# Post-norm attention and an int8 product: last heads joined by transfers, one more chunk in single steps

## The chip, the cores and the metric

The kernel runs on one core of a Trainium2 chip. The metric is device microseconds of one launch; the median of three runs of the kernel before is 1008.3 us (1007.88 to 1009.81). Engines as the profile calls them: PE (TensorE, matmuls; PEld its weight loads), DVE (VectorE), ACT (ScalarE), POOL (GpSimd), SP (SyncE, which issues all the transfers here).

## The reference

The input `x` has shape (2, 2048, 256), with 16 heads of width 16.

```python
Q, K, V = proj(Wq), proj(Wk), proj(Wv)            # x @ W.T, split into heads
O = flash_attention(Q, K, V, block 128, causal)   # online softmax, float32
x = layernorm(x + O @ Wo.T)                       # over the 256 features
# quantised product: integers of both sides, scales put back on
lhs_scale = max(absmax over a token, 1e-12) / 127
rhs_scale = max(absmax over a column, 1e-12) / 127
y = (round(x / lhs_scale) @ round(rhs / rhs_scale)) * lhs_scale * rhs_scale
x = layernorm(x + y)
```

## The kernel before

**Groups and steps.** Four heads of one batch are a group; there are eight groups, four for each batch, and they run one after the other. In a group the 2048 queries are cut into four chunks of 512, and a chunk meets the keys in blocks of 128, only those at or before it. That makes 4 + 8 + 12 + 16 = 40 steps (chunk c, block kb), numbered from 0 in each group; `NS` is 40 and `FIRST[c]` = 0, 4, 12, 24 is a chunk's first step. In the last four steps of a chunk the block lies on the diagonal, and the widths are 512, 384, 256 and 128. A step makes four score products (one for each head, into one of three PSUM banks `ps_score`), four exponentials on ScalarE into `PR` (L1003), and, two steps later (`LAG`), the values product into `ps_acc` (L734), whose row for each head also gives the sum of the exponentials.

**Items.** The maximum that each query subtracts is found ahead. TensorE makes scores into `ps_max`, VectorE reduces them (L1072, 1.06 us in the mean); such a piece is an item. Groups one to six make the items of the group that follows (80 each, a few of their own); the seventh makes 88 and the eighth none. `quota` (L164) writes down how many items are done after each score of a group. It goes through the steps with a price for each product and for the end work due in that step, and takes the highest pace at which all items still fit.

**A chunk's end.** When a chunk's last values are in `ps_acc`, ScalarE copies them to `accS` (`copy_acc`, L987), after the fourth exponential of the next chunk's second step. In groups one to seven SP stores these heads to HBM. When the four groups of a batch are through, a chunk's end work can be done: normalise all 256 rows by the inverse sums, project with `Wo`, add `x`, first layernorm, quantise, transpose, integer product, scale, add, second layernorm, store. It is done in halves of 256 tokens. `ENDS` = 8 chunks are numbered m = 0 to 7 over both batches and 16 halves e = 0 to 15.

**Two ways of doing the end work.** The first three chunks (`SOON = 3`) run one group after another beside the attention of the second batch: project, turn and product go through the score banks, ScalarE copies the results out and scales, GpSimd multiplies, and the VectorE steps are single instructions, one in each step (`SOON_DUE`, `gap=1`). The fourth chunk and the whole second batch run late, in the last group (`LATE_DUE`, `gap=0`): banks of `ps_max`, which has no items then; VectorE reads the projection in PSUM, and does all the instructions of a part in one step.

**The joined chunks.** Chunks 4 to 7 (`JOINED`) need the last group's own four heads. Those never go to HBM. The other twelve heads are loaded into `o_in(m)` (192 of the 256 rows; the last 64 rows of the second half are empty). For the last four heads TensorE sums the exponentials by token out of `accS` (`token_sums`, L879), VectorE inverts (`invert_last`, L1215), TensorE spreads the inverses over the rows (`spread_inverses`, L891), VectorE multiplies `accS` in place (`normalise_last`, L1222). The projection (`project`, L854) then has three products for each 128 tokens: 128 rows, 64 rows, and `accS` with `wo_last` (weights in the places of the spread-out heads). For chunk 7 the first two run ahead and `finish_projection` (L904) adds the third.

**What sets the order.** All instructions stand in program order on their engine; a wait stops all that is behind it. The lists `HALF_START`, `CHUNK_DUE` and the `..._DUE` tables give, for each part, the step at which each engine does it. `COPIED` holds the steps at which the copies of the joined chunks are made. In the last group `between_scores` (L775) puts a part of the projection behind each score, the token sums and spreads and the turn behind the first score of a step, the product behind the third, halves of the values behind the second and fourth.

Of the kernel before, what the change touches and what calls it, by code (L numbers as in the profile page):

```python
# [26 lines left out]
P = 128  # L27
# [7 lines left out]
HG = 4  # L35
# [26 lines left out]
def build(nc, x, wq, wk, wv, wo, ffn, out):  # L62
    B, T, D = x.shape
    DH = D // HEADS
# [4 lines left out]
    HALVES = D // P  # L69
    GR = HG * DH  # L70
# [32 lines left out]
    SOON = 3  # L103
# [6 lines left out]
    JOINED = range(CHUNKS, ENDS)  # L110
    COPIED = [LAST_GROUP + FIRST[c] + 1 for c in range(1, CHUNKS)] + [ALL - 1]
    HALF_START = [at for at in SOON_START for s in range(2)] + [LAST_GROUP, LAST_GROUP + 2] + \
        [at for k in COPIED[:-1] for at in (k + 2, k + 4)] + [ALL + 1, ALL + 2]
# [3 lines left out]
        for at in ((-16, -13, -11, -4), (-14, -11, -6, 1), (-13, -9, 2, 8), (-8, -4, 6, 14), (5, 9, 21, 29))]  # L117
# [15 lines left out]
    JOIN_DUE = dict(LATE_DUE, spread=0, normalise=0, project0=1, project1=1)  # L133
    LAST_DUE = dict(LATE_DUE, spread=0, normalise=0, project0=-2, project1=-2, finish=1)
    DUE = [SOON_DUE[e % 2] if e < SOON_HALVES else LATE_DUE if e // 2 not in JOINED else JOIN_DUE if e < 2 * ENDS - 2
# [11 lines left out]
    def joins_due(k):  # L147

        return [m for m in JOINED if HALF_START[2 * m] - 1 == k]

# [111 lines left out]
    with ExitStack() as ctx:  # L262
# [91 lines left out]
        e_token = sem("sums_by_token")  # L354
        e_spread = sem("inverses_spread")
# [40 lines left out]
        joined = lambda m: m - JOINED[0]  # L396
# [36 lines left out]
        with nc.Block() as block:  # L433
            @block.sync
            def _(sp):
# [43 lines left out]
                def end_parts(k):  # L479
                    for m in chunks_due(k, "sums_in"):  # L480
                        sums_in(m)
                    for m in chunks_due(k, "sums_back"):
                        sums_back(m)
                    for m in chunks_due(k, "load"):
                        load(m)
                    for e in due(k, "store"):
                        store_result(e)
# [40 lines left out]
                def load(m):  # L528
# [5 lines left out]
                    for h in range(HALVES):  # L534
# [6 lines left out]
                        .then_inc(e_x[SLOT[m]], 16)  # L541

# [33 lines left out]
            def _(pe):  # L576
# [198 lines left out]
                def between_scores(k, j):  # L775


                    at = NS * (GROUPS - 1) + k
                    project(at, j // 2, j % 2)
                    if j == 0:  # L780
                        joins(at)
                        late_turn(at)
                    if j == 2:
                        late_product(at)
                    if j % 2:
                        values_half(*divmod(at - LAG, NS), j // 2)

# [66 lines left out]
                def project(k, t, h):  # L854


                    for e in late_due(k, f"project{t}"):
                        m, s = divmod(e, 2)
                        if t == 0 and h == 0:
# [3 lines left out]
                            if e == 2 * JOINED[0]:  # L863
                                pe.wait_ge(e_wo, 16 * HG)
                            if m in JOINED and m < ENDS - 1:
                                pe.wait_ge(e_last, LAST_STEPS * joined(m) + 3 + s)
                        at, n = s * HALF + t * P, half_rows(m, h)
# [4 lines left out]
                        last = h == HALVES - 1  # L872
# [31 lines left out]
                def finish_projection(e):  # L904
                    m, s = divmod(e, 2)
                    pe.wait_ge(e_last, LAST_STEPS * joined(m) + 3 + s)
                    for t in range(TPH):
# [25 lines left out]
            def _(act):  # L933
# [53 lines left out]
                def copy_acc(g, c):  # L987
# [3 lines left out]
                    else:  # L991
                        act.wait_ge(e_y, TPH * late(2 * (JOINED[c - 2] + 1)))
                    act.copy(accS[:, c % 2, :], ps_acc[:, :]).then_inc(s_accS, 1)  # L993

                def group(g):
                    for k, (c, kb) in enumerate(STEPS):
                        w = CH - skip(c, kb)
                        for j in range(HG):
# [6 lines left out]
                            if kb == 1 and j == HG - 1 and (g or c):  # L1005
                                copy_acc(g if c else g - 1, (c - 1) % CHUNKS)
# [424 lines left out]
```

## Time and profile before

| | |
|---|---|
| median of three runs | 1008.3 us |
| profiled execution | 1007.38 us, span 1005.7 us |
| busy share of the span | PE 94%, DVE 80%, ACT 72%, POOL 27% |
| mean granted clock of TensorE | 0.983 of full speed |
| groups one to eight, from first exponential to the next group's | 98.3, 98.7, 98.7, 102.9, 104.1, 104.1, 106.7, 121.5 us |
| from the last group's last exponential to the end | 29.8 us |

The group times are differences between the starts of ACT's exponentials (L1003) in the timeline; the last group goes to the end of its last one. In the rows below, a line of the windows gives start:end, length, busy time and instruction count of PE, PEld, DVE, ACT and POOL, granted clock, DMA share and GB/s. A line of the waits gives the waiting engine, tile and line, what released it, and total us, times and longest. A piece of the chain of waits, or of the timeline, begins with its start and its length in us. A line of the groups gives count, busy time, mean ns of one, and idle time ahead of it. A transfer line ends with KB each and the median us from issue to landing.

### The profile page before, as it was taken

Reading aid. Unit: us, or ns where it says so; the run is one execution under the profiler, and the core shown is the slowest. Engines: PE = TensorE matmul, PEld = TensorE weight load, DVE = VectorE, ACT = ScalarE, POOL = GpSimd, SP = SyncE. Lnnn points to the kernel's source line nnn. Section 1 sums busy time; section 2 is a strip of 40 time slices with the busy share of each in tenths; the row PEclk is TensorE's granted clock in tenths of the full one; section 3 lists DMA queues with packets and bytes.
Section 4 is the critical chain, followed back from the end, with each engine's and each line's share of the span. In section 5 each row is a group of like instructions: output and inputs, shape, how many; then the busy total and the mean of one; then the engine's idle time right before and its main releaser. Section 6 shows DMA issues by size and latency. Waiting matters only on the chain.

```text
span 1005.7 us, 41095 instructions
## 1 busy us (share of the span) xinstructions
PE 944.5 (94%) x18208; PEld 590.9 (59%) x18208; DVE 799.5 (80%) x1081; ACT 719.9 (72%) x1494; POOL 272.0 (27%) x443
## 2 busy tenths in 40 slices
PE   8989999999999999999999999999999999879993
PEld 5645556656765676566656675666666654444441
DVE  5488888887888788878889898999899899365426
ACT  3423458788788878887878877887787887757670
POOL 4433452102210221021213230333124212353322
PEclk9999999999999999999999999999999999989995
DMA  5565440002210220022302230124013114502101
GB/s 177 161 200 159 157 125 15 5 9 53 69 32 9 60 68 24 9 58 80 83 6 60 64 116 8 40 76 114 19 34 78 50 33 112 114 14 75 34 2 42
DMA packets 70865, 66.47 MB, mean 66 GB/s; under 512 B 14704, under 2 KB 65200, under 8 KB 70688
## 3 DMA queue, kind: packets, MB, share of 16 engines
q1 hardware_dynamic: 70688, 63.84, 22.8%
q8 instruction: 143, 2.34, 1.0%
q14 instruction: 34, 0.28, 0.1%
HBM read 42.43 MB, written 20.91 MB: 63 GB/s over the span
## 4 chain that ended last, share of the span: by engine, by line
PE 77%; DVE 10%; ACT 6%; SPq 3%; issue 2%; POOL 1%; DMA 1%; POOLq 0%; ACTq 0%; DVEq 0%
PE ps_acc L734 20%; PE ps_score L681 19%; PE ps_max L681 18%; DVE block_max L1072 6%; PE ps_score L604 5%; ACT PR L1003 4%; PE ps_score L611 3%; PE ps_max L824 2%; PE ps_max L679 2%; SPq L439 2%; PE ps_max L699 2%; PE ps_score L824 1%; ACT accS L993 1%; PE ps_acc L585 1%; DVE end_slots L1183 1%
## 5 line engine op out<-in xcount | busy, mean ns | idle before, releaser
L1072 DVE TENSOR_REDUCE block_max<-ps_max 128x2 f32<-128x1024 f32 (+3 forms) x640 | 654.3, 1059 | 113.3 <-PE ps_max L681 56.7
L1003 ACT ACTIVATE PR<-ps_score 128x512 f32<-128x512 f32 (+3 forms) x1280 | 627.2, 539 | 160.4 <-PE ps_score L681 141.7
L681 PE MATMUL ps_score<-QS,KS 99*32 99x512 bf16 (+3 forms) x5120 | 452.3, 350 | 3.3 <-ACT PR L1003 2.2
L734 PE MATMUL ps_acc<-PR,VG 128*32 128x256 f32 (+1 forms) x5104 | 367.7, 350 | 10.5 <-ACT accS L993 9.1
L681 PE MATMUL ps_max<-KS,QS 96*32 96x512 bf16 (+3 forms) x4544 | 335.1, 348 | 5.5 <-DVE block_max L1072 2.9
L681 PEld LDWEIGHTS ps_score<-QS,KS 99*32 99x32 bf16 x5120 | 169.4, 96 | 96.5 <-ACT PR L1003 22.5
L734 PEld LDWEIGHTS ps_acc<-PR,VG 128*32 128x32 f32 x5104 | 170.2, 110 | 83.7 <-ACT PR L1003 16.2
L681 PEld LDWEIGHTS ps_max<-KS,QS 96*32 96x32 bf16 x4544 | 138.5, 96 | 88.4 <-DVE block_max L1072 37.7
L1318 POOL TENSOR_SCALAR_AFFINE_SELECT PR<-PR 128x512 f32<-128x512 f32 x128 | 82.8, 647 | 284.3 <-ACT PR L1003 284.1
L699 PE MATMUL ps_max<-mask_q,ident_b 128*32 128x96 bf16 (+3 forms) x1808 | 99.1, 200 | 0.0
L699 PEld LDWEIGHTS ps_max<-mask_q,ident_b 128*32 128x32 bf16 x1808 | 60.7, 97 | 10.0
L1326 POOL CAST max_parts<-neg_max 16x128 bf16<-16x128 f32 (+1 forms) x30 | 8.9, 297 | 195.1 <-ACT neg_max L985 193.1
L604 PE MATMUL ps_score<-PR,wT 128*128 128x512 f32 x128 | 60.3, 597 | 0.8 <-ACT neg_max L963 0.8
L945 ACT CAST end_slots<-ps_score 128x512 bf16<-128x512 f32 x32 | 18.7, 585 | 56.7 <-PE ps_score L604 56.7
L1305 POOL TENSOR_TENSOR end_slots<-PR,end_slots 128x512 bf16<-128x512 f32 x32 | 37.0, 1155 | 78.3 <-ACT end_slots L950 78.3
L679 PE MATMUL ps_max<-KS,QS 96*128 96x512 bf16 (+3 forms) x144 | 35.9, 345 | 7.1 <-DVE block_max L1072 7.0
L604 PEld LDWEIGHTS ps_score<-PR,wT 128*128 128x128 f32 x128 | 23.3, 190 | 20.6 <-issue 18.0
L1355 POOL TENSOR_SCALAR var_eps<-moments 128x2 f32<-128x2 f32 x32 | 7.4, 231 | 86.3 <-DVE moments L1178 86.3
L611 PE MATMUL ps_score<-wT,PR 128*128 128x256 f32 x128 | 30.0, 381 | 0.0
L1172 DVE BATCH_NORM_STATS2 stats<-end_slots 128x6 f32<-128x256 f32 x48 | 19.0, 417 | 12.0 <-POOL end_slots L1374 11.8
L1121 DVE TENSOR_TENSOR PR<-ps_score,end_slots 128x512 f32<-128x512 f32 x32 | 21.7, 683 | 8.0 <-ACT end_slots L945 6.9
L679 PEld LDWEIGHTS ps_max<-KS,QS 96*128 96x128 bf16 x144 | 13.3, 97 | 24.3 <-DVE block_max L1072 13.1
(125 smaller groups left out, 558.5 us busy)
## 6 DMA issues: line engine op xcount, KB each, us to landing
QS<-qparts SPq DMA_DIRECT2D x192, 64.0 KB, 2.4
KS<-kparts SPq DMA_DIRECT2D x192, 64.0 KB, 2.3
qparts<-end_slots SPq DMA_DIRECT2D x16, 384.0 KB, 3.8
kparts<-end_slots SPq DMA_DIRECT2D x16, 384.0 KB, 3.1
PR<-in_L_attn_x SPq DMA_DIRECT2D x8, 512.0 KB, 4.3
heads_out<-accS SPq DMA_DIRECT2D x112, 32.0 KB
end_slots<-in_L_attn_x SPq DMA_DIRECT2D x6, 512.0 KB, 7.5
out_y<-end_slots SPq DMA_DIRECT2D x12, 256.0 KB, 2.1
```

Source lines behind the costliest of these rows:

```text
L604: m = pe.matmul(bank, wT[:, w, mh, nh * P:nh * P + P], xT[:, n % 2, mh, :], start=mh == 0, stop=mh == HALVES - 1)
L611: m = pe.matmul(bank[:, t * D:t * D + D], xT[:, n % 2, mh, tile * P:tile * P + P], wT[:, 2, mh, :], start=mh == 0, stop=mh == HALVES - 1)
L679: return pe.matmul(bank[:, 0:w], stack, moving, start=True, stop=stop)
L681: m = pe.matmul(bank[t * QW:t * QW + QW, 0:w], stack[:, t * QW:t * QW + QW], moving, start=True, stop=stop)
L699: m = pe.matmul(bank[r:r + QW, w - P + r:w], ident_b[:, r:r + QW], mask_q[:, r:P], start=False, stop=True)
L734: m = pe.matmul(ps_acc[EYE * j:EYE * j + EYE, a:b], VG[:, kb, j, :], PR[:, k % 4, j, a - s:b - s], start=kb == 0 and a == 0, stop=k == LAS ...
L824: y = pe.matmul(out[r:r + QW], stack[:, r:r + QW], moving, start=start, stop=stop)
L1003: act.activation(PR[:, k % 4, j, 0:w], ps_score[:, bank_of(use), 0:w], ACT.Exp, scale=SCALE).then_inc(s_exp, 1)
L1072: dve.tensor_reduce(block_max[:, h * PAIR:h * PAIR + PAIR, i, b], ps_max[:, slot_at:slot_at + PAIR, 0:w], AX.X, ALU.max).then_inc(s_reduce ...
L1121: dve.tensor_tensor(rest[:, q % RESTS, :], ps_score[:, u % 3, :], parts[:, n % 2, u, 0, :], ALU.subtract)\
L1305: pool.tensor_tensor(parts[:, n % 2, u, 2, :], rest[:, q % RESTS, :], parts[:, n % 2, u, 1, :], ALU.subtract).then_inc(part3, 1)
L1318: pool.affine_select(out=block, in_=block, compare_op=ALU.is_ge, fill=0.0, base=0, pattern=[[0, HG], [1, P]], channel_multiplier=-1).then_ ...
```

## The change

- `SOON` is 4: the fourth chunk of the first batch takes the way of the first three. It starts at step 26 of the seventh group and ends at step 23 of the last one. The plan of the items counts this work.
- The joined chunks 4, 5 and 6 start their halves five and seven steps after the step of the copy, where it was two and four. Token sums stay one step after it; both halves are spread two steps after it and normalised three steps after it. Then SP copies the four heads by four transfers of 16 x 512 from `accS` to the empty rows of `o_in(m)` (`join_heads`), and the projection, which waits for these (`e_join`), has two products of 128 rows for each 128 tokens. Its two tiles are made in two steps, where it was one.
- In the last group the turn stands behind a step's fourth score, and token sums and spreads at the end of the step.
- `copy_acc` follows the third exponential of its step, where it was the fourth, in all groups. In the last group its wait for the buffer is for the transfers, where it was for the projection.
- The loads of chunk 7 come five steps later, and its weights' wait moves to `finish_projection`.

```diff
-    SOON = 3
+    SOON = 4
...
-    HALF_START = [at for at in SOON_START for s in range(2)] + [LAST_GROUP, LAST_GROUP + 2] + \
-        [at for k in COPIED[:-1] for at in (k + 2, k + 4)] + [ALL + 1, ALL + 2]
+    HALF_START = [at for at in SOON_START for s in range(2)] + \
+        [at for k in COPIED[:-1] for at in (k + 5, k + 7)] + [ALL + 1, ALL + 2]
...
-        for at in ((-16, -13, -11, -4), (-14, -11, -6, 1), (-13, -9, 2, 8), (-8, -4, 6, 14), (5, 9, 21, 29))]
+        for at in ((-14, -11, -6, 1), (-13, -9, 2, 8), (-8, -4, 6, 14), (5, 9, 26, 33))]
...
-    JOIN_DUE = dict(LATE_DUE, spread=0, normalise=0, project0=1, project1=1)
+    JOIN_DUE = [dict(LATE_DUE, spread=-3, normalise=-2), dict(LATE_DUE, spread=-5, normalise=-4, join=-4)]
...
-        return [m for m in JOINED if HALF_START[2 * m] - 1 == k]
+        return [m for m in JOINED if COPIED[joined(m)] + 1 == k]
...
+                    for e in due(k, "join"):
+                        join_heads(e // 2)
...
+                def join_heads(m):
+
+                    sp.wait_ge(e_last, LAST_STEPS * (joined(m) + 1))
+                    for j in range(HG):
+                        r = P - GR + j * DH
+                        sp.dma_start(o_in(m)[r:r + DH, HALVES - 1, :], accS[EYE * j:EYE * j + DH, m % 2, :])\
+                            .then_inc(e_join, 16)
...
-                    if j == 0:
-                        joins(at)
-                        late_turn(at)
                     if j == 2:
                         late_product(at)
+                    if j == 3:
+                        late_turn(at)
                     if j % 2:
                         values_half(*divmod(at - LAG, NS), j // 2)
+                    if j == 3:
+                        joins(at)
...
-                                pe.wait_ge(e_last, LAST_STEPS * joined(m) + 3 + s)
-                        at, n = s * HALF + t * P, half_rows(m, h)
+                                pe.wait_ge(e_join, 16 * HG * (joined(m) + 1))
+                        at, n = s * HALF + t * P, half_rows(m, h) if m == ENDS - 1 else P
...
-                        y = tiled(rows, o_in(m)[0:n, h, at:at + P], wT[0:n, 3, h, :], h == 0, last and m not in JOINED)
-                        if last and m in JOINED:
-                            y = tiled(rows, accS[:, m % 2, at:at + P], wo_last[:, :], False, True)
-                        if last:
+                        y = tiled(rows, o_in(m)[0:n, h, at:at + P], wT[0:n, 3, h, :], h == 0, h == HALVES - 1)
+                        if h == HALVES - 1:
                             y.then_inc(e_y, 1)
...
-                        act.wait_ge(e_y, TPH * late(2 * (JOINED[c - 2] + 1)))
+                        act.wait_ge(e_join, 16 * HG * (c - 1))
...
-                            if kb == 1 and j == HG - 1 and (g or c):
+                            if kb == 1 and j == HG - 2 and (g or c):
                                 copy_acc(g if c else g - 1, (c - 1) % CHUNKS)
```

## Rows read from the trace of the kernel before

**Rows 1.** The page, part 4: shares of the chain that ended last, by engine.

```profile
PE 77%; DVE 10%; ACT 6%; SPq 3%; issue 2%; POOL 1%; DMA 1%; POOLq 0%; ACTq 0%; DVEq 0%
```

**Rows 2.** Windows: second, sixth, seventh group, seventh's end, last in thirds, tail.

```profile
239.20:337.90 98.70, 96.34 (x2184) 62.93 (x2180) 82.56 (x84) 80.36 (x168) 17.13 (x37) 1.00 0.15 41
643.60:747.70 104.10, 101.74 (x2288) 66.74 (x2292) 93.13 (x125) 84.38 (x180) 29.38 (x53) 1.00 0.22 60
747.70:854.40 106.70, 103.55 (x2300) 63.56 (x2300) 100.42 (x127) 84.91 (x177) 28.37 (x51) 1.00 0.28 72
812.10:854.40 42.30, 41.32 (x849) 22.49 (x841) 41.16 (x46) 31.92 (x63) 6.66 (x12) 1.00 0.33 79
854.40:884.70 30.30, 26.06 (x513) 15.10 (x515) 12.75 (x37) 21.67 (x47) 12.69 (x21) 1.00 0.43 95
884.70:922.80 38.10, 32.63 (x560) 16.74 (x560) 24.56 (x72) 22.59 (x47) 15.02 (x21) 0.87 0.19 51
922.80:975.90 53.10, 48.72 (x852) 24.12 (x844) 22.86 (x69) 41.51 (x90) 16.29 (x24) 0.97 0.07 22
975.90:1005.70 29.80, 12.68 (x122) 7.67 (x120) 17.01 (x54) 3.01 (x5) 10.11 (x16) 0.66 0.11 36
```

**Rows 3.** Waits of all engines in the last group, 854.4 to 975.9.

```profile
ACT PR L1003 <- PE ps_score L681: 34.2, 45, 4.9
...
PE ps_max L899 <- DVE last_sums L1220: 4.0, 1, 4.0
```

**Rows 4.** The chain of waits, 882 to 904: first and last VectorE piece.

```profile
889.80 0.77 DVE stats L1172 x2
...
902.92 0.26 DVE last_sums L1220
```

**Rows 5.** Groups of instructions by line, 854.4 to 975.9.

```profile
L824 PE MATMUL ps_max<-wo_last,accS 128*32 128x256 f32 x96 | 7.7, 391 | 0.0
...
L1051 ACT ACTIVATE V<-V 128x512 bf16<-128x512 f32 x4 | 2.6, 649 | 0.3 <-DVE V L1212 0.3
...
L1226 DVE TENSOR_TENSOR accS<-accS,ps_max 128x256 f32<-128x256 f32 x6 | 2.5, 420 | 20.3 <-PE ps_max L899 20.3
```

**Rows 6.** ScalarE's timeline, 953 to 964.

```profile
955.06 5.99 ACT L1003 ACTIVATE PR<-ps_score 128x512 f32<-128x512 f32 x12 [1.19 <-PE ps_score L681]
```

**Rows 7.** Line 1003 in the last group: shortest/median/longest ns, stretch, shapes.

```profile
L1003 ACT ACTIVATE PR<-ps_score x160: 272/597/727, 854.4 to 975.6; 128x512 f32<-128x512 f32 x112, 128x384 f32<-128x384 f32 x16, 128x256 f32<-128x256 f32 x16, 128x128 f32<-128x128 f32 x16
```

**Rows 8.** SyncE's timeline, 860 to 872: store of heads, last load issued.

```profile
860.32 1.91 SPq L456 DMA_DIRECT2D heads_out<-accS  x4
...
870.83 0.58 SPq L540 DMA_DIRECT2D end_slots<-in_L_attn_x  x1
```

**Rows 9.** Transfers of the whole run.

```profile
QS<-max_parts SPq DMA_DIRECT2D x96, 4.0 KB, 1.7
```

**Rows 10.** Transfers of the stretch 850 to 885.

```profile
V<-in_L_attn_x SPq DMA_DIRECT2D x1, 512.0 KB, 9.2
...
QS<-max_parts SPq DMA_DIRECT2D x3, 4.0 KB, 6.5
```

**Rows 11.** The chain of waits from 249 to 253.5.

```profile
250.38 0.24 PE ps_acc L734 x2
...
251.01 0.59 ACT accS L993
...
251.73 0.64 PE ps_acc L734 x8
```

**Rows 12.** Waits before the last group, 140.9 to 854.4.

```profile
PE ps_acc L734 <- ACT accS L993: 9.1, 21, 0.6
```

**Rows 13.** VectorE's timeline, 962 to the end.

```profile
973.65 0.75 DVE L1172 BATCH_NORM_STATS2 stats<-end_slots 128x6 f32<-128x256 f32 x2 [7.44 <-POOL end_slots L1374]
...
974.60 0.84 DVE L1248 SCALAR_TENSOR_TENSOR end_slots<-ps_max,lscale,ffn_scale 128x256 f32<-128x256 f32 x2
```

More of the change, by code:

```diff
@@ L110, in build @@
     JOINED = range(CHUNKS, ENDS)
+    joined = lambda m: m - JOINED[0]
     COPIED = [LAST_GROUP + FIRST[c] + 1 for c in range(1, CHUNKS)] + [ALL - 1]
-    HALF_START = [at for at in SOON_START for s in range(2)] + [LAST_GROUP, LAST_GROUP + 2] + \
-        [at for k in COPIED[:-1] for at in (k + 2, k + 4)] + [ALL + 1, ALL + 2]
+    HALF_START = [at for at in SOON_START for s in range(2)] + \
+        [at for k in COPIED[:-1] for at in (k + 5, k + 7)] + [ALL + 1, ALL + 2]
     soon_chunk = lambda at: dict(sums_in=at - 17, sums_back=at - 14, load=at - 7, outputs=at - 2)
@@ L132, in build @@
                     take=7, product=8, scale=9, residual2=10, rstd2=12, store=14)
-    JOIN_DUE = dict(LATE_DUE, spread=0, normalise=0, project0=1, project1=1)
     LAST_DUE = dict(LATE_DUE, spread=0, normalise=0, project0=-2, project1=-2, finish=1)
-    DUE = [SOON_DUE[e % 2] if e < SOON_HALVES else LATE_DUE if e // 2 not in JOINED else JOIN_DUE if e < 2 * ENDS - 2
+    JOIN_DUE = [dict(LATE_DUE, spread=-3, normalise=-2), dict(LATE_DUE, spread=-5, normalise=-4, join=-4)]
+    DUE = [SOON_DUE[e % 2] if e < SOON_HALVES else LATE_DUE if e // 2 not in JOINED else JOIN_DUE[e % 2] if e < 2 * ENDS - 2
            else LAST_DUE for e in range(2 * ENDS)]
@@ L354, in build @@
         e_token = sem("sums_by_token")
+        e_join = sem("last_heads_joined")
         e_spread = sem("inverses_spread")
@@ L395, in build @@
         LAST_STEPS = 4
-        joined = lambda m: m - JOINED[0]
         banks_of = lambda m: ps_score if m == ENDS - 1 else ps_max
@@ L862, in project @@
                             pe.wait_ge(e_res, e - 1)
-                            if e == 2 * JOINED[0]:
-                                pe.wait_ge(e_wo, 16 * HG)
                             if m in JOINED and m < ENDS - 1:
-                                pe.wait_ge(e_last, LAST_STEPS * joined(m) + 3 + s)
-                        at, n = s * HALF + t * P, half_rows(m, h)
+                                pe.wait_ge(e_join, 16 * HG * (joined(m) + 1))
+                        at, n = s * HALF + t * P, half_rows(m, h) if m == ENDS - 1 else P
                         rows = ps_max[:, s, t * D:t * D + D]
@@ L871, in project @@
                             continue
-                        last = h == HALVES - 1
-                        y = tiled(rows, o_in(m)[0:n, h, at:at + P], wT[0:n, 3, h, :], h == 0, last and m not in JOINED)
-                        if last and m in JOINED:
-                            y = tiled(rows, accS[:, m % 2, at:at + P], wo_last[:, :], False, True)
-                        if last:
+                        y = tiled(rows, o_in(m)[0:n, h, at:at + P], wT[0:n, 3, h, :], h == 0, h == HALVES - 1)
+                        if h == HALVES - 1:
                             y.then_inc(e_y, 1)
@@ L906, in finish_projection @@
                     pe.wait_ge(e_last, LAST_STEPS * joined(m) + 3 + s)
+                    if s == 0:
+                        pe.wait_ge(e_wo, 16 * HG)
                     for t in range(TPH):
```

## The prediction

> **What bounds the kernel now.** I read the page first: the chain that ended last is 77% TensorE, and VectorE is next with 10% [rows 1]. That is an average over stages, so the table of windows comes next, cut where a group's first exponential starts [rows 2]. The second group takes 98.7 us with TensorE busy for 96.3. The sixth, which also carries the end work of one chunk of the first batch, takes 104.1 with 101.7 busy. The seventh makes all maxima of the eighth as well: 106.7 us, TensorE 103.6 and VectorE 100.4; in its last 42.3 us VectorE is busy for 41.2, as busy as TensorE. The eighth has no maxima items at all and is still the longest: 30.3 + 38.1 + 53.1 = 121.5 us, with ScalarE busy for 85.8 of them. It ought to be the shortest, so I look there.
>
> The waits of that stretch [rows 3] say that ScalarE stood 34.2 us for scores that TensorE had not made; TensorE in turn stood for VectorE, 4.0 us in one wait. The chain of waits shows why [rows 4]: from 889.8 to 903.2 it runs through VectorE alone, steps of the first batch's fourth chunk and of the first joined chunk in one row, and only then may TensorE spread the inverses of the second joined chunk. Its scores stand behind that in program order, so they stop too. The mean granted clock there is 0.87 [rows 2]: (1 − 0.87) / 0.5 × 38.1 = 9.9 us at 1.2 GHz. After the last exponential come 29.8 us of the last chunk's own latency [rows 2].
>
> **The change part by part.**
>
> *1. The last group.* Four things go. The fourth chunk's late steps leave the head of this group: the projection, and half one up to its rounding, move into the seventh group; the rest is spread in single instructions over steps 0 to 23 here. Token sums move from ahead of their step's second score to its end, behind the copy. Both halves' inverses are spread and normalised two and three steps after the copy, and the projection follows two steps later, so TensorE meets a finished result. And the projection loses the third product per tile: 96 matmuls, 7.7 us of busy TensorE [rows 5]. What is left is what ScalarE needs. Where it has scores in store, twelve 512-wide exponentials take 5.99 us, 0.50 each [rows 6]. The group has 112 such: 56; the 48 narrower ones I put at 0.33 on average, between 0.27, the shortest of the 160 [rows 7], and 0.50: 16. Three copies, six integer conversions and six copies of turned integers (takes) of the joined chunks, at the 0.65 of a conversion [rows 5], make 9.8; the fourth chunk's two conversions, two takes and four scalings of half that size 3.9. Sum 86. This agrees with the 85.8 now. On it come steps in which TensorE needs longer than ScalarE. A step's own matmuls are a little short of ScalarE's time; a product of a tile is 7.7 / 12 = 0.64 us, and two such, or token sums, or spreads lift some 18 steps above it by my estimate of 0.6 to 0.8 us, 13 us in all, of which the three score banks hide a part: 7. The tail of the group (the last chunk's partial projection beside short scores) is 1.5.
>
> Then the new waits. The projection of a joined chunk waits on TensorE for four transfers; behind it stand all scores. From the spread: two VectorE products at 0.42 [rows 5], four issues on SP, 1.9 us for the four from the same buffer now [rows 8], a landing. No such landing is in the trace. The nearest are the small rows of maxima, 1.7 us over the run [rows 9], but 6.5 in this stretch, where a large load takes 9.2 [rows 10]. With 2 us, near the 1.7, the heads are there 0.8 + 1.9 + 2.0 = 4.7 us after the spread, just when two steps at about 2.2 us end; with 6.5 they are 4.8 us late. The first joined chunk has the 6.5 against it, since its issue follows soon on the loads that SP now ends at 871.4 [rows 8]; ahead of the others no load stands so near. I take 2 us for the first, 0.5 for each other. One more wait: the second joined chunk's spread of half two needs the residual add of the chunk before, and VectorE stands ahead of that at the inversion of the new token sums, then norms and rounds half a chunk; I put 1.5 us on it after the banks' cover. Sum 86 + 7 + 1.5 + 3 + 1.5 = 99; as single terms are rounded up I take 98. The group gives back 121.5 − 98 = **23.5 us**; bounds: 14 (all waits at the upper rows) to 31.
>
> Here a rule speaks against the change. In this trace the clock fell after TensorE had stood waiting, and its share at the lower level cost the middle third [rows 2]. The Trainium skill, "TensorE: Matmul & The Clock Gate", section "Part 1: The HAM clock gate", says that a monitor sets the array's clock from how busy it has recently been. By that, a last group bounded by ScalarE could lose the full clock again; in the last 53.1 us, where ScalarE is busy for 41.5, the mean is 0.97, so the trace shows little of that. It is a rival below.
>
> *2. The seventh group.* A whole chunk of end work costs a group 104.1 − 98.7 = 5.4 us of span and 93.1 − 82.6 = 10.6 us of VectorE [rows 2]. The fourth chunk brings its first half's VectorE steps (5.3) and all four projections here, into the 42.3 us in which VectorE is 97% busy. The plan of the items answers by making up to three of them earlier, which moves some 3 us of VectorE into steps where it has 7 to 10% left. Below 2 us it can't come, since VectorE's 105.7 us then need 99% of the span; above 8 only if each added step also stops TensorE. I take **+4.5 us**.
>
> *3. The earlier copy of the accumulator*, in every group. In the second group TensorE's values of a chunk's last step end at 250.62, ScalarE has the fourth exponential to do first, the copy starts at 251.01, and TensorE begins the next chunk's values at 251.73 [rows 11]. TensorE waited for this 9.1 us in 21 waits up to 854.4 [rows 12], some three in a group. The copy may start when the values are done, 0.35 us earlier in this case; 21 × 0.35 to 0.43 = 7.4 to 9.1 is the most that can come back. Against it the fourth exponential is 0.6 us later, and the copy at a group's first steps gains nothing; where VectorE bounds, nothing comes either. I take **−5 us**; bounds −9 and +3 (28 copies, 0.1 us lost at each).
>
> *4. The tail.* The third joined chunk starts three steps later, so its last scaling, its statistics and its norms fall behind the last exponential, ahead of the last chunk's residual add in VectorE's order. Now one scaling (974.60, 0.84 us) and one pair of statistics (973.65, 0.75) are done before it [rows 13]; those two are new there, 1.6 us, and between them an add of GpSimd, which lies mostly under the last chunk's own products on TensorE. I take **+1.5 us**; bounds 0 and 4.
>
> *At nothing:* the stores, loads and sums that move by a few steps (SP has gaps of many us between them), and the normalisations, which VectorE did already and for which it has the time (60.2 us busy of 121.5 [rows 2]).
>
> Sum: −23.5 + 4.5 − 5 + 1.5 = −22.5. The profiled execution took 1007.4, so 984.9; the runs' median is 0.9 above it, 1008.3, and the forecast is made against that: **985.8 us**.
>
> **Rivals.**
> - *The best of each* (0.11): ScalarE alone sets the last group, 92 us; copies bring 8.5, the seventh group costs 3, the tail 0.5: 1008.3 − 29.5 − 8.5 + 3.5 = 974. For it: nothing in this group but order holds ScalarE. Against: TensorE's heavy steps are still there.
> - *VectorE's row only moves* (0.13): spreads and quantising now stand behind inversions that wait for TensorE at the end of a step. Three such waits of 4 us, as the 4.0 of [rows 3]: 997.8. For it: the engine's order still mixes chunks. Against: the fourth chunk's steps are no longer in it in one row.
> - *VectorE bounds the seventh group* (0.11): the steps stop items, items stop scores, and the earlier copy gives nothing: 12 instead of 4.5, 0 instead of −5: 998.3. For it: 97% busy. Against: TensorE hid most of the same work in the sixth group.
> - *The clock falls* (0.06): two stretches like the 9.9 us now, in which TensorE does half the work, twice 5 us: 995.8. By the rule of the Trainium skill named above it would go this way. Against: 0.97 in the stretch that is nearest to ScalarE's pace [rows 2].
> - *The change does less than it says* (0.05): the earlier copy makes ScalarE wait for values with a finished score at hand, 0.5 us at 28 copies instead of −5: 1004.8.
> - *The heads land late* (0.04), the other side: transfers queue behind the loads. At a landing of 9.2 us each projection waits 7.5 us, three times 22 instead of 3; TensorE's standstill takes the clock, 5 us for each chunk: 1020 us. It decides from a wait of 8.5 us a chunk at the full clock, (22.5 + 3) / 3, and of 3.5 us if the clock goes too. For it: 9.2 and 6.5 in this stretch [rows 10]. Against: only the first chunk has loads ahead of it.
>
> **How the numbers follow.** The forecast has 0.50; its own range is 977 to 993. Range 973 to 999: outside are part of the best case, the last two rivals and the ends of the others, under 0.2. Three quarters of the 0.04, and 0.01 of the rest, are slower: 0.04; within 0.2% (about 2 us, what a measurement here can't tell from none) 0.03, faster 0.93.
>
> **What would show it.** Last group near 98 us, no VectorE row of 13 us in the chain, ScalarE's waits for scores cut from 34 to about 10: part 1. The projection's wait for the transfers: 0.5 to 2 us. The seventh group at 109 to 113 us. Waits for the copy under 4 us before the last group, and groups two and three about 1 us shorter. From last exponential to end 30 to 33. Wrong it is if the last group stays above 110, or if groups one to six grow.

## The result, and the profile after

The changed kernel takes 998.1 us (median of 4 runs, 995.6 to 999.5) against 1008.5 of the kernel before on the same chip: a ratio of 0.989 [0.987, 0.992]. Timed once more beside other kernels, it takes 995.1 us, a ratio of 0.986 [0.983, 0.988]. The forecast was 985.8, a gain of 22.5 us; it gained 10 to 14. The profiled run took 995.6, the fastest of the four, and its stages are compared with those of the profiled run before.

The table of windows of the changed kernel, with the columns of [rows 2]: second, sixth, seventh and last group, the last one in thirds, tail.

```profile
238.26:336.16 97.90, 96.66 (x2186) 62.02 (x2182) 82.54 (x84) 79.94 (x169) 17.17 (x37) 1.00 0.17 41
640.00:741.40 101.40, 100.11 (x2260) 67.06 (x2256) 91.67 (x123) 82.69 (x178) 28.44 (x51) 1.00 0.22 60
741.40:853.50 112.10, 108.02 (x2374) 67.61 (x2377) 102.77 (x138) 84.91 (x181) 29.38 (x53) 1.00 0.26 69
853.50:960.60 107.10, 94.31 (x1729) 52.23 (x1719) 56.34 (x155) 84.41 (x184) 44.78 (x66) 0.97 0.23 60
853.50:876.80 23.30, 20.82 (x381) 10.80 (x371) 8.46 (x25) 20.14 (x48) 12.55 (x20) 0.93 0.53 126
876.80:909.50 32.70, 26.77 (x508) 16.08 (x512) 14.98 (x43) 23.28 (x51) 11.74 (x16) 1.00 0.06 17
909.50:960.60 51.10, 46.72 (x848) 25.35 (x840) 32.91 (x89) 41.00 (x88) 20.49 (x31) 0.97 0.21 56
960.60:993.90 33.30, 13.77 (x142) 8.23 (x140) 19.68 (x60) 3.60 (x6) 11.49 (x17) 0.65 0.09 32
```

From first exponential to first exponential, groups one to six are together 6.2 us shorter than before (the second 97.9, was 98.7; the window of the sixth here is cut 1.5 us late). The seventh is 5.4 longer (112.0, was 106.7), the last 14.4 shorter (107.1, was 121.5), the tail 3.5 longer. −6.2 + 5.4 − 14.4 + 3.5 = −11.7, and 1007.4 − 11.7 = 995.7. The forecast for this run was 1007.4 − 22.5 = 984.9, so it missed by 10.7 us. Most of that lies in the last group (98 forecast, 107.1 measured: 9.1 us); the tail is 2.0 over its forecast, the seventh group 0.9 over, and groups one to six 1.2 better.

Look at TensorE in that group. Before, it was busy for 107.4 of 121.5 us (the sum of three lines of [rows 2]) and idle for 14.1. Now it is busy for 94.3 of 107.1 and idle for 12.8. Nearly all of the gain is work that TensorE no longer has or does at a higher clock (mean 0.97, before 0.94); its standing changed little. (One profiled run is not the whole picture. In a second one of the changed kernel the group took 106.7 us, busy for 96.5 at a clock of 0.95, idle for 10.3. In a third, of the kernel of the experiment "The tail" below, which is the same up to the end of this group, it took 109.5: busy for 98.6 at a clock of 0.92, idle for 10.8. So a difference of less than 3 us between two profiled last groups shows nothing by itself.) The waits of that group, with the columns of [rows 3]:

```profile
ACT PR L1012 <- PE ps_score L692: 18.2, 29, 3.1
...
DVE end_slots L1192 <- POOL rstd L1367: 16.8, 4, 11.1
DVE last_sums L1227 <- PE ps_max L894: 8.9, 3, 6.9
...
PE ps_score L692 <- ACT PR L1012: 3.3, 5, 1.4
...
PE ps_max L836 <- DMA V<-accS: 2.5, 2, 2.2
PE ps_max L906 <- DVE V L1281: 2.4, 1, 2.4
...
ACT V L1060 <- DVE V L1221: 1.9, 1, 1.9
...
PE ps_max L836 <- DMA end_slots<-accS: 1.2, 1, 1.2
```

ScalarE's wait for scores fell from 34.2 us [rows 3] to 18.2, where about 10 was expected. TensorE stands mostly for three things: the heads' transfers (2.5 + 1.2), a residual add of VectorE ahead of a spread (2.4), and ScalarE, which has all three score banks still to read (3.3).

The chain of waits at the first joined chunk shows the new path: two products of VectorE, four issues of SP, the landing, the projection.

```profile
872.70 0.42 DVE accS L1235
...
873.13 0.43 DVE accS L1235
...
873.58 0.57 SPq L551
...
874.19 1.22 SPq L551
...
875.45 0.59 SPq L551
...
876.08 2.71 DMA V<-accS
...
878.93 0.64 PE ps_max L836 x8
```

From the first product to the projection it is 6.2 us; TensorE stood for 2.2 of them. The chain at the spread of the second joined chunk, and TensorE's timeline at its end:

```profile
891.64 0.18 DVE last_sums L1227
891.85 0.25 DVE last_sums L1229
892.10 0.57 DVE V L1192 x2
...
894.11 1.93 DVE V L1215 x2
896.06 0.43 DVE V L1221
896.49 0.61 DVE V L1281
```

```profile
897.24 0.64 PE L906 MATMUL ps_max<-ident,last_sums 128*32 128x128 f32 x16 [2.38 <-DVE V L1281]
```

VectorE takes up the inversion (L1227) when the token sums are there, and only behind it the norms, the quantising and the residual add (L1281) of the chunk before, which frees the bank. The spread of half two stands for the add, and the scores stand behind the spread. The row of VectorE steps of [rows 4], 13.4 us, is now 5.5.

Waits before the last group (columns as in [rows 12]), where the wait for the copy was 9.1 us in 21:

```profile
PE ps_acc L745 <- ACT accS L1002: 2.2, 5, 0.5
```

### The profile page after: what moved, and what is told of

Read it like the earlier page. It is cut to its first block, busy times and chain, and to the rows that moved or that the text cites. A ratio compares the mean times of both kernels' runs of the same rounds, so it can differ in the third digit from the quotient of the medians.

```text
span 993.9 us, 40924 instructions
## 1 busy us (share of the span) xinstructions
PE 936.7 (94%) x18112; PEld 590.9 (59%) x18112; DVE 800.5 (81%) x1077; ACT 716.8 (72%) x1502; POOL 275.1 (28%) x447
## 4 chain that ended last, share of the span: by engine, by line
PE 76%; DVE 11%; SPq 5%; ACT 3%; issue 2%; DMA 2%; POOL 0%; POOLq 0%; DVEq 0%; ACTq 0%
PE ps_acc L745 20%; PE ps_score L692 19%; PE ps_max L692 18%; DVE block_max L1081 7%; PE ps_score L615 5%; SPq L440 3%; PE ps_score L622 3%; PE ps_max L690 2%; ACT PR L1012 2%; PE ps_score L836 2%; PE ps_max L710 2%; PE ps_max L836 1%; DVE end_slots L1192 1%; PE ps_acc L596 1%; SPq L457 1%
## 5 line engine op out<-in xcount | busy, mean ns | idle before, releaser
L1012 ACT ACTIVATE PR<-ps_score 128x512 f32<-128x512 f32 (+3 forms) x1280 | 619.7, 541 | 142.2 <-PE ps_score L692 126.5
L1192 DVE TENSOR_SCALAR end_slots<-end_slots,moments,rstd 128x256 f32<-128x256 f32 x48 | 24.4, 523 | 17.4 <-POOL rstd L1367 17.4
L615 PEld LDWEIGHTS ps_score<-PR,wT 128*128 128x128 f32 x128 | 23.3, 190 | 20.9 <-issue 18.2
```

The source lines that it names most:

```text
L615: m = pe.matmul(bank, wT[:, w, mh, nh * P:nh * P + P], xT[:, n % 2, mh, :], start=mh == 0, stop=mh == HALVES - 1)
L1012: act.activation(PR[:, k % 4, j, 0:w], ps_score[:, bank_of(use), 0:w], ACT.Exp, scale=SCALE).then_inc(s_exp, 1)
L1192: dve.tensor_scalar(dst[:, at, :], src[:, at, :], moments[:, z, which, at, 0:1], rstd[:, z, which, at:at + 1], ALU.subtract, ALU.mult).the ...
```

## The experiments

The lengths of groups and steps below are differences between the starts of the exponentials in each run's timeline.

**The copy alone.** The kernel before with only the earlier copy:

```diff
-                            if kb == 1 and j == HG - 1 and (g or c):
+                            if kb == 1 and j == HG - 2 and (g or c):
```

> The kernel before with the earlier copy of the accumulator alone (after the third exponential). Theory A (the changed kernel's first seven groups lost 6.3 us, and apart from the seventh's new work this is all the copy): TensorE's waits for the copy before the last group fall from 9.1 to about 2 us, and the time is 1008.4 - 6.5 = 1002. Rival B (most of those 6.3 us come from something else in the change, since the later fourth exponential gives back what the copy brings): under 2 us, 1006 to 1008.

Measured: 1001.5 us, a ratio of 0.992 [0.991, 0.994]. Groups two and three 97.9, the last 120.1; TensorE's wait for the copy before the last group fell to 1.8 us. Theory A stands, and the rival, that the index costs as much as it brings, fell: 7.4 of the 10 to 14 us that the change gained are this one index.

**The fourth chunk and the joined chunks apart.** Three kernels start from the changed one. The first keeps the fourth chunk's early way and takes the joined chunks back to the third product, to the spread one step ahead of the projection, and to the old places in the step (the later start stays):

```diff
-    JOIN_DUE = [dict(LATE_DUE, spread=-3, normalise=-2), dict(LATE_DUE, spread=-5, normalise=-4, join=-4)]
+    JOIN_DUE = dict(LATE_DUE, spread=0, normalise=0, project0=1, project1=1)
...
-                        y = tiled(rows, o_in(m)[0:n, h, at:at + P], wT[0:n, 3, h, :], h == 0, h == HALVES - 1)
+                        y = tiled(rows, o_in(m)[0:n, h, at:at + P], wT[0:n, 3, h, :], h == 0, last and m not in JOINED)
+                        if last and m in JOINED:
+                            y = tiled(rows, accS[:, m % 2, at:at + P], wo_last[:, :], False, True)
```

> The changed kernel with the old way of joining: inverses spread in the step of the projection, a third product out of the copied heads, turn and token sums behind the first score; fourth chunk still in single steps, halves still five and seven steps after the copy. Theory A (what the last group lost beside its work are stops of TensorE in its program order): the old stops are back, about 2 us for each of six spreads and 1.2 for each of three token sums, and 5 us of third products: last group 107 + 16 less 4 of transfer waits = 119, time about 1010. Rival B (the group is at the limit of its work): only the third products are added, last group 112, time 1003.

The second takes only the transfers away and puts the third product back; spreads stay early:

> The changed kernel without the transfers: the projection waits for the normalised heads and adds the third product out of them; all steps as in the changed kernel. Theory A: the stops for the transfers' landing (2.2 + 0.3 + 1.2 us) go and twelve products of 0.43 us come, of which part is hidden by ScalarE: last group 107 to 109, time 998 to 1000. Rival B (work is the limit): last group 112, time 1003.

The third keeps all of the new joins, and the fourth chunk goes late:

```diff
-    SOON = 4
+    SOON = 3
...
-    HALF_START = [at for at in SOON_START for s in range(2)] + \
+    HALF_START = [at for at in SOON_START for s in range(2)] + [LAST_GROUP, LAST_GROUP + 2] + \
```

> The changed kernel with the fourth chunk late in the last group as before (two halves at its first steps), joins by transfers and earlier copy kept. Theory A: the seventh group is back at about 105.5; the last keeps the row of VectorE steps of the fourth chunk in its first third, but TensorE no longer stops for it at each join: 115, time 998.1 - 6.5 + 8 = 1000. Rival B (chunk four's place doesn't matter, its work only moves): last group 112.5, time 997 to 998.

To close the square, a fourth kernel, run later, has the old joins and the fourth chunk late, so that against the copy alone only the start of the joined halves (and chunk 7's loads) moves:

> Late fourth chunk and old joins as before, the earlier copy, and the joined halves starting five and seven steps after the copy instead of two and four. With the runs so far the last group takes 120.1 us (copy alone), 110.3 (fourth chunk in single steps, old joins, later start), 106.3 (late fourth chunk, new joins, later start), 107.1 (changed kernel). Theory A (what cost the old last group its time was VectorE's row of the fourth chunk's and the first joined chunk's steps, and three steps of distance between them are enough): last group 108 to 111, time 991 to 994. Rival B (the joining by transfers, with the spread ahead of the projection, is what frees the group): last group 114 to 118, time 998 to 1001.

Measured (us; group lengths, busy time of TensorE in the last group and its idle rest, all from the profiled run; the time is the median):

| kernel | seventh | last | TensorE busy + idle | time |
|---|---|---|---|---|
| before | 106.7 | 121.5 | 107.4 + 14.1 | 1008.5 |
| copy alone | 106.3 | 120.1 | 106.3 + 13.8 | 1001.5 |
| later start: old joins, fourth chunk late | 106.3 | 116.5 | 107.1 + 9.4 | 999.1 |
| old joins, fourth chunk early | 112.0 | 110.3 | 102.9 + 7.5 | 999.2 |
| third product, fourth chunk early | 112.0 | 111.4 | 102.2 + 9.2 | 1001.2 |
| new joins, fourth chunk late | 106.3 | 106.3 | 95.8 + 10.5 | 990.5 |
| changed: new joins, fourth chunk early | 112.0 | 107.1 | 94.3 + 12.8 | 998.1 |

Of the four kernels between the copy alone and the changed one, the later start came as its rival B had it (114 to 118, 998 to 1001), and the third product nearly so (111.4 for 112, 1001.2 for 1003). For the other two neither theory stood: the old joins with the fourth chunk early were 1.7 us shorter in the last group and 4 us faster than rival B, and the new joins with it late were 6 to 9 us shorter in that group than either theory. The square says more than each. With the old joins, moving the fourth chunk takes 6.2 us from the last group and adds 5.7 to the seventh: nothing. With the new joins it takes nothing from the last group (106.3 and 107.1) and adds 5.7 to the seventh: a loss, and without it the kernel takes 990.5 us, 0.983 [0.981, 0.986]. The joins bring 10.2 us of the last group with the fourth chunk late, 3.2 with it early. The early spreads without the transfers bring nothing that can be seen (110.3 and 111.4). What pays is that the third product goes: TensorE's busy time falls by 7.9 us, its standing grows by 3.6, about what it stands for the transfers, and the group falls from 111.4 to 107.1 (medians 1001.2 and 998.1). The later start by itself shortens the last group by 3.6 us, but the tail grows from 29.0 to 32.7, and the two profiled runs are equal (999.4 and 999.5). The windows of the last group with the third product (a profile of its slowest run, 1005.8 us, of which the fourth group has 105.3):

```profile
859.63:971.00 111.37, 102.20 (x1825) 53.13 (x1817) 56.20 (x155) 84.69 (x184) 45.12 (x66) 0.97 0.22 54
```

The windows of the kernel with the new joins and the fourth chunk late, seventh and last group:

```profile
741.67:847.98 106.31, 103.61 (x2300) 63.68 (x2300) 100.41 (x127) 84.73 (x176) 28.29 (x51) 1.00 0.27 72
847.98:954.28 106.30, 95.78 (x1793) 54.89 (x1793) 59.91 (x170) 83.71 (x180) 42.67 (x64) 0.98 0.22 60
```

TensorE's busy time in the seventh group is 103.6 here and 108.0 in the changed kernel: 4.4 us more. The groups of instructions of the last group show what moved, first in this kernel, then in the changed one:

```profile
L836 PE MATMUL ps_max<-wT,end_slots 128*32 128x256 f32 x128 | 9.8, 380 | 1.2 <-issue 0.9 <-DMA end_slots<-accS 0.4
```

```profile
L836 PE MATMUL ps_max<-wT,end_slots 128*32 128x256 f32 x64 | 4.9, 380 | 1.2 <-DMA end_slots<-accS 1.2
```

The fourth chunk's 64 projection matmuls, 4.9 us, are the bulk of it. TensorE is the busiest engine of both groups, so they cost about 5 us where they go. Where they were, they should save about as much; with the old joins they did. In this pair TensorE's busy time in the last group fell by only 1.5 us (95.8 to 94.3, the clock lower) and its standing grew by 2.3.

**VectorE's order.** In the changed kernel the inversion of the token sums goes to the end of VectorE's end work:

```diff
-                    for m in joins_due(k):
-                        invert_last(m)
                     for t in range(TPH):
                         for e in due(k, f"norm2_{t}"):
...
                     for e in due(k, "aggr1"):
                         moments_of(e, 0)
+                    for m in joins_due(k):
+                        invert_last(m)
```

> The changed kernel with VectorE inverting the token sums at the end of its step's end work, where it was at its head, so that it no longer waits there for TensorE with ready work behind it. Theory A (the 9 us by which the last group is over my 98 are stops in program order): TensorE's 2.4 us wait for the residual add at step 15 of the last group goes, steps 14 and 15 take 6 us instead of 9.0, last group 105. Rival B (the group is full of work): steps 14 and 15 shorten, but the following lengthen by as much; last group 107.

A single run: 995.8 us with the last group at 104.4; steps 14 and 15, where the spread stood, take 6.4 us instead of 9.0. The seventh group is 113.7 in this run, with no edit in it, so the time by itself would have hidden the effect. TensorE's wait for the residual add is gone from its waits, and 104.4 lies below all three last groups without the edit (106.7 to 109.5). The reading of the spread's stop is right.

**GpSimd's order.** In the last group GpSimd does its end work ahead of a step's mask:

```diff
+                        if g == GROUPS - 1:
+                            end_parts(NS * g + k)
                         if kb >= TPC * c:
                             mask(g, k)
```

> The changed kernel with GpSimd's end work of a step ahead of its mask in the last group, where it was behind. Theory A: VectorE's waits for GpSimd's inverse deviations (16.8 us, the longest 11.1, behind a mask that waits for ScalarE at step 20) shrink to under 8, ScalarE's conversion at step 24 finds its numbers ready, steps 24 to 27 take 11.5 us instead of 14.4; last group 104.5. Rival B: masks now come late, values stop for them, last group 107 or more.

A single run: 997.9 us, the last group 109.9. VectorE's wait for `rstd` fell only from 16.8 to 14.0 us in 4, and steps 24 to 27 took 16.0 us instead of 14.4; without the edit they take 14.4 to 15.5 from run to run, and the group 106.7 to 109.5. So theory A fell: the edit gains nothing. But it hardly shortened the wait, so what the wait costs is not shown.

**The first projection a step later.**

```diff
+    FIRST_JOIN = [dict(JOIN_DUE[s], project0=1, project1=2 - s) for s in range(2)]
```

> The changed kernel with the first joined chunk's projection one step later (first half; the second half makes both tiles in one step). Theory A: TensorE's stop of 2.2 us for the transfers at step 10 goes, step 10 takes 2 us instead of 4.55, and about 1 us comes back in the step with two tiles: last group 105.5. Rival B: 107.

A single run: 995.4 us, the last group 106.4. Step 10 went from 4.6 to 1.4 us and step 11 from 2.0 to 3.4; steps 10 to 13 together from 12.4 to 10.8. But in the second and third profiled run without this edit (see above) steps 10 to 13 took 11.2 and 13.7 us, so the wait is worth 0.4 to 2.9 us, by the run beside which it is put.

**The tail.** The third joined chunk's second layernorm falls behind the last chunk's rounding:

```diff
+    LATER_END = (dict(stats2_0=17, stats2_1=17, aggr2=17, rstd2=18, norm2_0=19, norm2_1=19, store=20),
+                 dict(stats2_0=16, stats2_1=16, aggr2=16, rstd2=17, norm2_0=19, norm2_1=19, store=20))
```

> The changed kernel with the second layernorm of the third joined chunk put behind the last chunk's rounding on VectorE, where it stood ahead of the last chunk's residual add. Theory A (the tail grew from 29.8 to 33.3 us because these steps delay the last chunk's): the tail is 30.5, time 995.5. Rival B (it grew because the projection, product and token sums of two chunks meet on TensorE at half clock): 33.

A single run: the tail 31.1 us, as theory A has it nearly (30.5), where it was 33.0 and 33.3. Two of the kernels below, with the same edit and the fourth chunk late, have 31.1 again. The time was 999.8, since the seventh group took 115.1 and the last 109.5 in that run, before the edit has any part in it.

**Together.** The last two edits, the inversion behind, and the second joined chunk's conversion a step later; with the fourth chunk late (first, with the first projection later too) and early (second), and the changed kernel again beside them:

> The changed kernel with the fourth chunk late in the last group (seventh group as before), inversion behind the other end work of its step, first joined projection a step later, conversions and all that follows of the second joined chunk a step later, second layernorm of the third joined chunk behind the last chunk's rounding. Theory A (the stops add up): last group 106.3 - 2.5 - 1 - 1.5 = 101.3, tail 31, time 990.5 - 7 = 983.5. Rival B (the group is full; one stop takes another's place): last group 104 to 106, time 987 to 988.

> The changed kernel with its fourth chunk in single steps as it is, and with inversion behind, the later conversions of the second joined chunk and the later second layernorm of the third. Theory A: last group 107.1 - 2.7 - 1.5 = 103, tail 31, seventh group 112 to 114 as now: time 998.1 - 6.5 = 991.6. If the fourth chunk's place is worth nothing to the last group, this stays 7 to 9 us above the kernel with it late. Rival B: 996.

> The changed kernel once more, beside the others on one chip: 998 by its four runs. The last group's step 10 took 4.55 us in its profile and 5.9 in two others that are the same up to there: by the transfers' landing the last group should vary between 107 and 110, and with it the time between 995 and 1000.

Measured: 989.6 us (0.980 [0.977, 0.983]), 990.4 (0.982 [0.979, 0.984]) and 995.1. In the repeat of the changed kernel step 10 took 3.4 us and the last group 106.7, just below the 107 to 110 expected. With the fourth chunk early the last group falls to 102.3 us (TensorE busy 91.6 + 10.7 idle, granted clock 1.00), as theory A had it: of the 9.1 us that were missing, VectorE's order and the late conversion hold 4.8. Their places show it: steps 14 and 15 take 6.4 us instead of 9.0, steps 24 to 27 12.4 instead of 14.4. With it late the group stayed at 107.0, longer than either theory had it. TensorE's timeline of that kernel says why:

```profile
875.03 1.08 PE L911 MATMUL ps_max<-ident,last_sums 128*32 128x128 f32 x32 [2.08 <-DVE last_sums L1234]
```

The inversion of the first joined chunk now stood behind the fourth chunk's row of VectorE steps, and the spread waited for it: steps 7 and 8 took 9.2 us, in the kernel without this edit 5.6. So a last version puts only that inversion back in front, with the first projection in its old step:

```diff
+                        if m == JOINED[0]:
+                            invert_last(m)
...
+                        if m > JOINED[0]:
+                            invert_last(m)
```

> The changed kernel with three edits: the fourth chunk goes its old late way (SOON = 3); VectorE inverts the token sums at the end of its end work for the second and third joined chunk, but ahead of it, as in the changed kernel, for the first; the second joined chunk's parts from its conversion on come a step later, and the third one's second layernorm falls behind the last chunk's rounding. Theory A (in best_a the inversion of the first joined chunk stood behind the fourth chunk's row of VectorE steps, where TensorE waited 2.1 us for it and the clock fell after, and that took what the other edits gave): the steps 0 to 9 of the last group fall from 29.8 back to 26.3, the last group to 102 to 104, and the time to 985 to 988. Theory B (best_a's long steps are run-to-run variation, or the fourth chunk's row itself): steps 0 to 9 stay above 28, the time at 989 to 991.

> The same kernel as join_soon3 (the changed kernel with the fourth chunk late), beside best_c on one chip. Theory A: last group 106.3 with 26.3 in steps 0 to 9 again, 990 to 991 us, 3 to 5 us behind best_c. Theory B: within 1.5 us of best_c, steps 0 to 9 between 26 and 30 from one run to another.

Measured: 988.9 us (0.980 [0.978, 0.982]) and 989.8 (0.983 [0.980, 0.985]). Steps 0 to 9 fell from 29.8 to 26.2 us, as theory A had it, and the last group to 104.9, a little above its 102 to 104. The time is at the edge of theory B's, and the two kernels can't be told apart by it: the one without the edits has a last group of 105.7 in this run. Both beat the kernel before; neither stood beside the changed one on a chip, as 989.6 and 990.4 did (995.1).

This pair also answers what I had written down for the fourth chunk: if its place were worth nothing to the last group, the kernel with it early would stay 7 to 9 us behind. It does not: 990.4 against 989.6 on one chip. The last groups of the last version (fourth chunk late) and of the one with it early, both at the full clock:

```profile
849.41:954.28 104.87, 94.51 (x1793) 53.91 (x1793) 61.49 (x170) 83.28 (x180) 42.68 (x64) 1.00 0.24 61
856.52:958.85 102.33, 91.61 (x1729) 50.99 (x1721) 56.34 (x155) 84.06 (x184) 44.69 (x66) 1.00 0.24 62
```

In these two profiles the last group gives back 2.5 us (TensorE's busy time 2.9) where the seventh takes 6.0 more (106.3 and 112.3). The 2.5 is within the spread of one profile, but the times say the same: in none of these pairs does the fourth chunk's move gain time, and beside the later edits its loss can't be seen any more.

## Why the prediction was wrong

1. **The last group, forecast −23.5, measured −14.4: the step that failed.** The sum was built on ScalarE: 86 us of its own work, 7 for TensorE's heavy steps, 6 of new waits, less 1 for rounding up. ScalarE's work was right: busy for 84.4. But ScalarE was not what bounds the group: it stood for 22.7 us, 18.2 of them for scores, where the sum left it 98 − 86 = 12. The term that failed is the 7 us for steps in which TensorE needs longer, with the estimate under it that a step's own matmuls are a little short of ScalarE's time; by busy time alone TensorE needs 94.3 − 84.4 = 9.9 us more than ScalarE, and it stands besides. Built on TensorE the sum begins at 107.4 [rows 2] − 7.7 for the third product [rows 5] − 4.9 for the fourth chunk's projection = 94.8, and 94.3 was measured. That they agree so closely is partly luck, since the other two runs have 96.5 and 98.6 at a lower clock. My 98 thus left 3 us for all of TensorE's standing, which was 14.1 before. It came to 12.8 in one run and 10.3 in another, and no version with the new joins came below that. The 14.4 lies within the bounds of 14 to 31 by luck: the 14 was built on transfers that land after 6.5 us, and they landed after 2.0 to 2.9.
2. **The fourth chunk's part of that term was worth nothing.** I credited its departure from the head of the group. Moving it is a transfer of TensorE's work from one group that TensorE bounds to another, +5.4 to 5.7 us in the seventh; beside the new joins of the changed kernel the last group gives none of it back, and some 2.5 us, by one pair of profiles, beside the later edits. The forecast had the cost of the seventh group nearly right (+4.5; VectorE came to 102.7 us there, priced at 105.7) and paired it with a gain that the joins alone already have.
3. **The new waits were nearly right where they were priced.** Transfers: 3.7 us of TensorE's standing, forecast 3, the first the longest as forecast. The four issues took 2.4 to 3.3 us, where I took 1.9, and the landing 2.9, 2.0 and 2.4, where I took 2. The spread behind the residual add: 2.4, forecast 1.5. Not forecast was the conversion (ScalarE 1.9). That is the place of the rival "VectorE's row only moves", which came nearest in time (997.8); at 4.8 us its price is less than half of the 12 it was given, so it is right in the mechanism and does not explain the miss by itself. The rival "VectorE bounds the seventh group" is as near (998.3) by luck alone: it had 12 us for the seventh group and nothing for the copy, and 5.4 and −6.2 were measured.
4. **The copy, forecast −5, measured −6.2** in groups one to six, and −7.4 in all as a run by itself. The wait for it fell to 2.2 us, forecast under 4.
5. **The tail, forecast +1.5, measured +3.5**, within its bounds. VectorE's timeline of the changed kernel, after the last exponential at 960.6:

```profile
969.23 0.84 DVE L1257 SCALAR_TENSOR_TENSOR end_slots<-ps_max,lscale,ffn_scale 128x256 f32<-128x256 f32 x2
...
970.45 1.66 DVE L1192 TENSOR_SCALAR end_slots<-end_slots,moments,rstd 128x256 f32<-128x256 f32 x2
972.03 0.74 DVE L1181 BATCH_NORM_STATS2 stats<-end_slots 128x6 f32<-128x256 f32 x2
...
972.97 0.66 DVE L1281 TENSOR_TENSOR end_slots<-ps_max,end_slots 128x512 f32<-128x512 f32 x1
```

   The scaling and the statistics are the two that I counted (0.84 and 0.74); the norms between them took 1.66 more, ahead of the last chunk's residual add (L1281). I had named the norms and left them out of the sum. Moving the second layernorm took 2.2 us back in a run by itself.
6. **The clock did not fall in two of three runs.** That rival is not the cause of the miss in the profiled run, but the clock is not steady. Its mean in the last group, 0.94 before, was 0.97 and 0.95 in the two runs of the changed kernel and 0.92 in the one that differs only in the tail, where the group was the longest (109.5). It was 1.00 in the version with a last group of 102.3, so the missing stops and the full clock come together there; their shares are not separated.

What stays open: some 10 us in which TensorE stands in the last group of the best versions too; it is spread over many short waits (in the last version the longest is 2.0 us; ScalarE still waits for scores some 30 times), and no run with the new joins took more of it away. With the old joins and the fourth chunk early TensorE stood for 7.5 us, but was busy for 102.9.

## What to carry to other kernels

When the same engine is the busiest of two neighbouring stages, moving work between them gains nothing (here 6.2 us for 5.7 with the old joins, none for 5.7 with the new); remove the work (here 96 matmuls), or leave it. Make the sum of a stage on every engine's busy time, take the largest, and keep the idle time seen before on top unless each wait that goes has a name. When two edits remove the same stop, try each without the other: here, beside the new joins, the other edit had only its cost.

## What the runs showed of the hardware

VectorE's `TENSOR_SCALAR` instructions are long where GpSimd adds beside them. The pair of L1215 at 894.11 took 1.93 us, and GpSimd's add ran from 894.62 to 895.88; the same pair in the tail, with GpSimd idle, took 0.63. The pair of norms in the fence above, 1.66 us, lies over an add of GpSimd from 970.38 to 971.64. The Trainium skill, "SBUF — State Buffer", section "Who interferes with whom", says that the two engines share a pair of ports, that `tensor_scalar` is among the VectorE instructions that can take it, and that whichever engine issues first holds it for its whole instruction while the other is blocked; these rows agree, though no run took GpSimd's add away.

Issues on SP are not of one length: the four stores out of `accS` took 1.9 us to issue in [rows 8], and 1.7 to 3.1 over that whole run. The four transfers to a joined chunk took 3.1, 2.4 and 3.3 us in the changed kernel; why is not shown. The first of them:

```profile
873.58 3.09 SPq L551 DMA_DIRECT2D V<-accS  x4
```

And groups that no edit touches vary: with the earlier copy the fourth group took 101.0 to 102.6 us in most runs, 105.3 and 106.0 in two; the seventh with the fourth chunk early 111.3 to 115.1.
